# A softmax-attention block in eight wide steps in place of sixteen, and an output stage in another buffer

## The reference

```python
# recurrence
xp = silu(LN(x) @ W_in.T)
alpha, beta = sigmoid(xp @ W_alpha.T + b), sigmoid(xp @ W_beta.T + b)
h_t = alpha_t * h_(t-1) + (beta * tanh(xp @ W_v.T + b_v))_t
x = x + (h * silu(h)) @ W_out
# heads within a position: H = 16, HD = 64
y = LN(x); h = rmsnorm(y)
q = h @ Wq + bq; kv = (h @ Wdown + bdown) @ Wup + bup
att = softmax(q_h . k_g / 8 over the 16 heads g)     # per position
u = y + (att @ v) @ Wo + bo
# experts: E = 8
h2 = rmsnorm(u); gate = softmax(h2 @ Wg + bg)
x = x + u + sum_e gate_e * (h2 @ We_e)
```

## Time and profile before

| | us |
|---|---|
| median of 3 runs | 3924.3 (3923.45 to 3926.99) |
| the profiled execution's own time | 3921.82 |
| its span on the slowest core | 3919.9 |
| spans of the 8 cores | 3892.3 to 3919.9 |
| PE busy | 2538.4 (65%) |
| DVE busy | 1510.3 (39%) |
| ACT busy | 875.7 (22%) |
| mean granted TensorE clock of the slowest core | 0.762 of full |

### The profile page before, as it was taken

The page is one execution under the profiler, slowest core; times in us unless marked ns, Lnnn a source line. Parts: engine busy times, 40 slices in busy tenths (PEclk is TensorE's granted clock), DMA queues, the critical chain, the costliest instruction groups (busy, mean ns, idle before and its releaser), DMA issues.

```text
span 3919.9 us, 36774 instructions; the slowest of 8 cores (3892.3 to 3919.9 us)
## 1 busy us (share of the span) xinstructions
PE 2538.4 (65%) x12352; PEld 1190.4 (30%) x12352; DVE 1510.3 (39%) x2201; ACT 875.7 (22%) x1642; POOL 79.9 (2%) x143
## 2 busy tenths in 40 slices
PE   3555766557774487645975459664696647965478
PEld 1222332223332233222432224332243223432234
DVE  1353323443334433344324533146332363234532
ACT  2232003321123201332023320242203411023210
POOL 0000000000000000000000000000000000000000
PEclk8756888657886688966888669785698757987579
DMA  8631681201321022300223003220042201412012
GB/s 169 143 83 43 129 193 65 86 5 75 135 108 43 22 86 108 129 22 22 108 108 108 22 22 129 108 86 22 22 150 86 108 1 40 154 65 86 1 65 108
DMA packets 44465, 319.80 MB, mean 82 GB/s; under 512 B 5048, under 2 KB 5304, under 8 KB 28928
## 3 DMA queue, kind: packets, MB, share of 16 engines
q0 software_dynamic: 35040, 283.53, 23.1%
q1 hardware_dynamic: 9248, 33.91, 2.2%
HBM read 301.07 MB, written 48.23 MB: 89 GB/s over the span
## 4 chain that ended last, share of the span: by engine, by line
PE 52%; DVE 19%; DMA 10%; issue 7%; ACT 7%; DVEq 4%; ACTq 1%; POOL 0%; POOLq 0%; SPq 0%
PE bank L1420 21%; PE bank L614 3%; PE bank L836 3%; PE bank L1137 3%; DMA w<-wscr 3%; DMA w<-we 3%; PE bank L1363 3%; PE bank L443 3%; PE bank L489 2%; DVE vpu L927 2%; DVE kpot L927 2%; DVE xph L1036 2%; DVE sstat L1026 2%; PE bank L965 2%; DVEq L1030 2%
## 5 line engine op out<-in xcount | busy, mean ns | idle before, releaser
L1420 PE MATMUL bank<-qpg,w 128*128 128x512 bf16 x4096 | 915.6, 388 | 77.0 <-DVE qpg L1393 42.2
L1420 PEld LDWEIGHTS bank<-qpg,w 128*128 128x128 bf16 x4096 | 406.8, 100 | 594.5 <-issue 131.6
L1393 DVE TENSOR_TENSOR qpg<-xph,ybuf 128x4096 bf16<-128x4096 bf16 x64 | 282.4, 4423 | 502.2 <-PE bank L1420 502.2
L1012 ACT ACTIVATE hfm<-bank,sstat 128x128 bf16<-128x128 f32 x512 | 146.0, 368 | 652.7 <-DVE sstat L987 641.6
L1437 ACT ACTIVATE acomb<-bank 128x512 f32<-128x512 f32 x64 | 38.2, 597 | 1133.3 <-PE bank L1420 1129.4
L1059 PE MATMUL bank<-cpb_s,xph 128*128 128x128 bf16 x512 | 74.9, 300 | 332.1 <-DVE xph L1036 308.9
L525 PE MATMUL bank<-xph,w 128*128 128x512 bf16 x512 | 133.1, 407 | 125.5 <-DMA w<-wscr 64.9
L614 PE MATMUL bank<-ln1g,w 128*128 128x512 bf16 x512 | 128.5, 418 | 97.2 <-DMA w<-wscr 74.6
L987 DVE TENSOR_REDUCE sstat<-bank 128x4 f32<-128x512 f32 x128 | 88.5, 692 | 235.9 <-PE bank L965 235.9
L912 PE MATMUL bank<-zb,wupb 64*128 64x512 bf16 x128 | 73.2, 584 | 156.0 <-DVE vpu L927 112.0
L927 DVE TENSOR_SCALAR kpot<-bank,cph_s 64x512 bf16<-64x512 f32 x128 | 95.1, 743 | 196.5 <-PE bank L912 192.6
(11 more groups left out here) (139 smaller groups left out, 3025.4 us busy)
## 6 DMA issues: line engine op xcount, KB each, us to landing
w<-wscr POOLq DMA_DIRECT2D x105, 2048.0 KB, 8.1
wscr<-w POOLq DMA_DIRECT2D x15, 2048.0 KB, 9.3
w<-we POOLq DMA_DIRECT2D x8, 2048.0 KB, 20.2
out<-tmstage SPq DMA_DIRECT2D x16, 1024.0 KB, 4.0
slotA<-x SPq DMA_DIRECT2D x4, 2048.0 KB
slotB<-x SPq DMA_DIRECT2D x4, 2048.0 KB, 12.7
w<-w_inT POOLq DMA_DIRECT2D x1, 2048.0 KB, 29.3
w<-w_aT POOLq DMA_DIRECT2D x1, 2048.0 KB, 23.0
```

Source lines behind the costliest of these rows:

```text
L1012: last_s = s.activation(out=p1_[bb % 4][:, g4 * 128:(g4 + 1) * 128], in_=bkS[:, g4 * 128:(g4 + 1) * 128], func=AF.Exp, bias=sstat[:, SG_[b ...
L1393: r = v.tensor_tensor(qpg[:, (e % 2) * 4096:(e % 2) * 4096 + 4096] .rearrange("p (c q) -> p c q", q=512), h2v[:, :, :], ybuf[:, e * 512:(e ...
L1420: last_pe = pe.matmul(bk[:, :], wslice(wbuf, kc, mc), qpg[:, (e % 2) * 4096 + kc * 512: (e % 2) * 4096 + (kc + 1) * 512], start=(e == 0 an ...
```

## The change

A step of the attention block takes 8 groups in place of 4, so there are 8 blocks `mm` (`NMAC = 8`) and 12 steps. The scores of a block fill two banks: 0 and 1, or 2 and 3. P transposes take banks 4 and 5, V transposes bank 6 alone, O bank 7 over its whole width. Maxima stay two instructions, one to a bank; exponentials stay one to a group. V copy, sums, reciprocals, multiply, P copy and O copy become one instruction for 8 groups. Scores wait for the exponentials two blocks back (three before) and for V copy of the block before (two blocks back before). `p1_` has three slots of 1024, `p1n_` and `p1t_` two, and `vlay_` moves to the second half of `ln1g`. `stage2` becomes the first half of `ybuf`; the waits for the output transfer of the tile before go from the two writers of `tmstage` (L390, L785) to the three writers of `ybuf`.

```diff
-    p1_ = [hfm[:, i * 512:(i + 1) * 512] for i in range(4)]
-    p1n_ = [xph2[:, i * 512:(i + 1) * 512] for i in range(4)]
-    p1t_ = [xph2[:, 2048 + i * 512: 2048 + (i + 1) * 512] for i in range(2)]
-    vlay_ = [xph2[:, 3072 + i * 256: 3072 + (i + 1) * 256] for i in range(4)]
+    p1_ = [hfm[:, i * 1024:(i + 1) * 1024] for i in range(3)]
+    p1n_ = [xph2[:, i * 1024:(i + 1) * 1024] for i in range(2)]
+    p1t_ = [xph2[:, 2048 + i * 1024: 2048 + (i + 1) * 1024] for i in range(2)]
+    vlay_ = [ln1g[:, 2048 + i * 512: 2048 + (i + 1) * 512] for i in range(4)]
...
-    stage2 = tmstage[:, :].bitcast(F32)
+    stage2 = ybuf[:, 0:2048]
...
                 s.wait_ge(s_ve.h, tok[("ln1nmr", t)])
                 if t > 0:
-                    osem, oval = tok[("out", t - 1, 1)]
-                    s.wait_ge(osem.h, oval)
+                    s.wait_ge(s_pe.h, tok[("h2T", t - 1, NCH - 1)])
...
                     s.wait_ge(s_pe.h, tok[("wbv", t, mc)])
+                    if mc == 0 and t > 0:
+                        osem, oval = tok[("out", t - 1, 1)]
+                        s.wait_ge(osem.h, oval)
...
-                if t > 0:
-                    osem, oval = tok[("out", t - 1, 1)]
-                    s.wait_ge(osem.h, oval)
                 for b in range(NBLK):
                     last_s = s.activation(out=tmstage[:, b * 1024:(b + 1) * 1024],
...
                 s.wait_ge(s_ve.h, tok[("bv", t, NCH - 1)])
+                if t > 0:
+                    osem, oval = tok[("out", t - 1, 1)]
+                    s.wait_ge(osem.h, oval)
                 for b in range(NBLK):
                     last_s = s.activation(out=ybuf[:, b * 1024:(b + 1) * 1024],
...
+            def emit_F1(mm):
+                bkS = [banks[2 * (mm % 2)], banks[2 * (mm % 2) + 1]]
+                bkV = banks[6]
...
+                    if mm < 2:
                         pe.wait_ge(s_se.h, tok[("qe", t, NCH - 1)])
                         pe.wait_ge(s_ve.h, tok[("kve", t, 15)])
...
                     else:
+                        pe.wait_ge(s_se.h, tok[("p1e", t, mm - 2)])
+                    if mm >= 1:
+                        pe.wait_ge(s_ve.h, tok[("vle", t, mm - 1)])
+                    for half in range(2):
+                        bk = bkS[half]
+                        pe.matmul(bk[:, :], QM, KM, start=True, stop=False)
+                        for g4 in range(4):
...
+                    for g8 in range(8):
+                        grp = mm * 8 + g8
+                        last_pe = pe.transpose(bkVb[:, g8 * 64:(g8 + 1) * 64],
...
+                    for half in range(2):
+                        r = v.tensor_reduce(
+                            sstat[:, SG_[mm % 2] + 4 * half:SG_[mm % 2] + 4 * half + 4],
+                            bkS[half][:, :].rearrange("p (g n) -> p g n", n=128),
+                            axis=AX, op=OP.max, negate=True)
...
+                    r = v.tensor_copy(vlay_[mm % 4][:, :],
+                                      bkV[:, :].bitcast(BF16)[:, 0:512])
...
+                    if mm >= 3:
+                        s.wait_ge(s_ve.h, tok[("ssum", t, mm - 3)])
+                    for g8 in range(8):
+                        half, g4 = g8 // 4, g8 % 4
                         last_s = s.activation(
+                            out=p1_[mm % 3][:, g8 * 128:(g8 + 1) * 128],
+                            in_=bkS[half][:, g4 * 128:(g4 + 1) * 128],
...
+                        p1_[mm % 3][:, :].rearrange("p (g n) -> p g n", n=128),
                         axis=AX, op=OP.add)
...
+                    r = v.tensor_copy(p1t_[mm % 2][:, :],
+                                      bkP[:, :].bitcast(BF16)[:, 0:1024])
...
+                        if g8 == 3:
+                            s_pe.inc(last_pe)
+                            tok[("avh", t, mm)] = s_pe.n
...
+                        bkO[:, 0:512].rearrange("p (g u i) -> p g u i", u=8, i=8))
...
+            NMAC = 8
+            for step in range(NMAC + 4):
...
                         if e == 0:
                             dwait(v, "d_y")
                             v.wait_ge(s_ve.h, tok[("ud", t)])
+                            if t > 0:
+                                osem, oval = tok[("out", t - 1, 1)]
+                                v.wait_ge(osem.h, oval)
```

More of the change, by code:

```diff
@@ L136, in build_program @@
     S_GMAX, S_SSUM, S_RSUM = 44, 48, 52
-    SG_ = [64 + 4 * i for i in range(4)]
-    SS_ = [80 + 4 * i for i in range(4)]
-    SR_ = [96 + 4 * i for i in range(4)]
+    SG_ = [64, 72]
+    SS_ = [80, 88]
+    SR_ = [96, 104]
     banks = [ctx.enter_context(nc.psum_tensor(f"bank{i}", [128, 512], F32))
@@ L960, in f_s1 @@
                     else:
[L961 to L968, removed]
+                        pe.wait_ge(s_se.h, tok[("p1e", t, mm - 2)])
[5 more added lines that the diff above has]
+                        for g4 in range(4):
+                            grp = mm * 8 + half * 4 + g4
+                            last_pe = pe.matmul(bk[:, g4 * 128:(g4 + 1) * 128],
+                                      q64[:, grp * 128:(grp + 1) * 128],
+                                      k64[:, grp * 128:(grp + 1) * 128],
+                                      start=False, stop=(g4 == 3))
                     s_pe.inc(last_pe)
-                    tok[("s1", t, bb)] = s_pe.n
+                    tok[("s1", t, mm)] = s_pe.n
                     bkVb = bkV[:, :].bitcast(BF16)
-                    for g4 in range(4):
-                        grp = bb * 4 + g4
-                        last_pe = pe.transpose(bkVb[:, g4 * 64:(g4 + 1) * 64],
+                    for g8 in range(8):
+                        grp = mm * 8 + g8
+                        last_pe = pe.transpose(bkVb[:, g8 * 64:(g8 + 1) * 64],
                                      v64[:, grp * 128:(grp + 1) * 128],
@@ L1008, in f_exp @@
                         dwait(s, "d_hfm")
-                    if bb >= 4:
-                        s.wait_ge(s_ve.h, tok[("ssum", t, bb - 4)])
-                    for g4 in range(4):
+                    if mm >= 3:
+                        s.wait_ge(s_ve.h, tok[("ssum", t, mm - 3)])
+                    for g8 in range(8):
+                        half, g4 = g8 // 4, g8 % 4
                         last_s = s.activation(
-                            out=p1_[bb % 4][:, g4 * 128:(g4 + 1) * 128],
-                            in_=bkS[:, g4 * 128:(g4 + 1) * 128],
+                            out=p1_[mm % 3][:, g8 * 128:(g8 + 1) * 128],
+                            in_=bkS[half][:, g4 * 128:(g4 + 1) * 128],
@@ L1055, in f_p1tT @@
                     else:
-                        pe.wait_ge(s_ve.h, tok[("p1te", t, bb - 2)])
+                        pe.wait_ge(s_ve.h, tok[("p1te", t, mm - 2)])
                     bkPb = bkP[:, :].bitcast(BF16)
-                    for g4 in range(4):
-                        last_pe = pe.transpose(bkPb[:, g4 * 128:(g4 + 1) * 128],
-                                     p1n_[bb % 4][:, g4 * 128:(g4 + 1) * 128], idb)
+                    for g8 in range(8):
+                        last_pe = pe.transpose(bkPb[:, g8 * 128:(g8 + 1) * 128],
+                                     p1n_[mm % 2][:, g8 * 128:(g8 + 1) * 128], idb)
@@ L1084, in f_av @@
                     elif t > 0:
                         pe.wait_ge(s_ve.h, tok[("G", t - 1, 7)])
-                    for g4 in range(4):
+                    for g8 in range(8):
                         for hl in range(2):
                             last_pe = pe.matmul(
-                                bkO[64 * hl:64 * hl + 64, g4 * 64:(g4 + 1) * 64],
-                                vlay_[bb % 4][:, g4 * 64:(g4 + 1) * 64],
-                                p1t_[bb % 2][:, g4 * 128 + hl * 64:
-                                             g4 * 128 + (hl + 1) * 64],
+                                bkO[64 * hl:64 * hl + 64,
+                                    (g8 % 8) * 64:(g8 % 8) * 64 + 64],
+                                vlay_[mm % 4][:, g8 * 64:(g8 + 1) * 64],
+                                p1t_[mm % 2][:, g8 * 128 + hl * 64:
+                                             g8 * 128 + (hl + 1) * 64],
@@ L1110, in f_ote @@
                     s_ve.inc(r)
-                    tok[("ote", t, bb)] = s_ve.n
+                    tok[("ote", t, mm)] = s_ve.n
                 block.vector(f_ote)
-            for step in range(16 + 4):
-                if step < 16:
+            NMAC = 8
+            for step in range(NMAC + 4):
+                if step < NMAC:
                     emit_F1(step)
                     emit_F2(step)
-                if step >= 2 and step - 2 < 16:
+                if step >= 2 and step - 2 < NMAC:
@@ L1119, in build_program @@
                     emit_B1(step - 2)
-                if step >= 4 and step - 4 < 16:
+                if step >= 4 and step - 4 < NMAC:
                     emit_B3(step - 4)
-                if step >= 3 and step - 3 < 16:
```

(3 more changed lines are left out.)

157 lines of the change are left out of this document (68 added, 89 removed).

## The result

The changed kernel takes 3841.58 us (median of nine runs), the kernel before 3922.37 us (ten runs): a ratio of 0.9793, 95% interval 0.9777 to 0.981. The prediction was 3841, range 3805 to 3868. The profiled execution took 3847.39 us; its cores' spans run from 3809.3 to 3845.4 us.

A forecast was written before the change was run, and what follows sets the result against it. The attention block was taken as a loop passing between VectorE and TensorE, neither engine the bound; 10.45 us less a tile, 83.6 in eight, took 3921.8 to 3838.2, plus 2.5 for the median: 3841, range 3805 to 3868.

The forecast's parts named there:

- VectorE's half: Attention block, steady step: VectorE's work from the maxima on takes 5.58 us, for 6.48 in two old steps.
- TensorE's half: Attention block, steady step: from the P copy's end to the next maxima 3.32 us, for 4.04 in two old steps.
- Head and tail: Attention block's start and end: maxima 7 at 54.18 us, then 18.20 to the output projection, 72.38 in all for 82.83.
- The added wait of scores 1 for V copy 0: Attention block's head: with one bank for V transposes, scores 1 wait for V copy 0 and start at 4.19 us.
- ScalarE: Attention block: eight exponentials take 2.3 us, covered, no scores delayed; otherwise each 1 us late costs 1 us a step.
- The output stage's move: Layer norm of the next tile: it loses its wait for the output DMA, gain nothing, covered by the sum over x.
- The total: Whole kernel: 83.6 us off the profiled 3921.8 gives 3838.2; the median stands 2.5 higher, so 3841; chance 0.80.
- a stage outside the block that changes length: Outside the attention block: any stage changing length was named as showing the prediction wrong; no size given.
- (a): Attention block: wider bursts release TensorE's clock, scores and PV get cheaper, 9 us a tile, so 3769; chance 0.10.
- (b): Attention block: everything doubles with the width, 1.6 us less a tile, 3911; 3896 if only VectorE doubles; chance 0.05.
- (c): Weight loads in each tile: a shorter block makes them meet and take twice as long, so 3979; chance 0.03.
- (d): Behind the attention block: another wait takes the gain and the time stays at 3924; chance 0.02.

The follow-up runs named there:

- the reordered wide kernel: The changed kernel with TensorE's scores and V transposes of step k+1 issued ahead of P transposes k-2 and PV k-3; ratio 0.942 to the kernel before.
- the last version: The reordered wide kernel with V copy and O copy moved from VectorE to ScalarE; ratio 0.9309 to the kernel before.
- the narrow kernel in the new order: The kernel before, sixteen narrow steps, with TensorE's scores and V transposes of block k+1 issued ahead of P transposes and PV; ratio 0.9556.

## Why the prediction was right, step by step

**VectorE's half.** Predicted 5.58 us, measured 5.59. The widened instructions came out as the two-size estimate had them. Groups of the changed kernel (line, operation, count, total busy and mean ns), which answer to the earlier trace rows:

```profile
L1040 DVE TENSOR_TENSOR xph<-hfm,sstat 128x1024 bf16<-128x1024 bf16 x64 | 78.4, 1225 | 8.4 <-issue 0.4
...
L1030 DVE TENSOR_REDUCE sstat<-hfm 128x8 f32<-128x1024 bf16 x64 | 77.4, 1210 | 0.0
...
L1115 DVE CAST tmstage<-bank 128x512 bf16<-128x512 f32 x64 | 43.9, 686 | 17.7 <-PE bank L1092 17.7
L1077 DVE COPY xph<-bank 128x1024 bf16<-128x1024 bf16 x64 | 43.6, 682 | 0.0
```

Multiply 1.225 us (estimated 1.22), sums 1.21 (1.21), O copy 0.686 and P copy 0.682 (0.69 each). That the fixed part is what was saved here is shown by the kernel with narrow VectorE instructions: 0.71 us a step for six instructions more. The Trainium skill (VectorE: DVE Perf Modes, the section on the TRN2 errata) says that VectorE operations reading SBUF pay a fixed extra latency in each instruction, and so many small ones pay it many times. The trace agrees that there is a fixed part, but not that it comes with reading SBUF: two narrow multiplies, which read SBUF, last 0.15 us longer than the wide one (2 x 0.69 and 1.23), two narrow P copies, which read PSUM, 0.16 longer (2 x 0.42 and 0.68), and by starts they cost 0.08 and 0.06 more.

**TensorE's half.** Predicted 3.32, measured 3.32, but that is luck: two terms were off by as much in opposite directions. PV to the next scores was twice the old 0.35, 0.71, and measured 0.57 (1287.05 to 1287.62): two PV bursts back to back cost less than two apart. Scores to the maxima was 2.25 (2.08 and the hand-over of 0.17), and measured 2.39 (1287.62 to 1290.01). The first half's four score matmuls are followed by the next mask matmul after 0.53 us; I had priced them at 0.40, the time until a V transpose follows.

**Head and tail.** From the first score matmul (1244.86), predicted then measured: maxima 0 at 2.25, 2.30; maxima 2 at 10.63, 10.50; maxima 4 at 27.48, 27.33; maxima 7 at 54.18, 54.05; tail 18.20, 17.98. The added wait of scores 1 for V copy 0 is there, and it is as long as worked out. Timeline of the changed kernel: start of the block, scores 1, the last maxima and the output projection, answering to the earlier trace rows:

```profile
1244.86 0.58 PE L964 MATMUL bank<-cpb_s 8*128 8x512 bf16 x1 [2.61 <-DVE vpu L929]
...
1248.93 0.58 PE L964 MATMUL bank<-cpb_s 8*128 8x512 bf16 x1 [1.45 <-DVE ln1g L999]
...
1298.91 0.69 DVE L990 TENSOR_REDUCE sstat<-bank 128x4 f32<-128x512 f32 x1 [3.31 <-PE bank L967]
...
1316.89 1.44 PE L1146 MATMUL bank<-tmstage,w 128*128 128x512 bf16 x3 [1.05 <-DVE tmstage L1115]
```

The block is 72.03 us, predicted 72.38. Scores 1 start 4.07 after the first, predicted 4.19, by a hand-over of 0.15 from the V copy's end (1248.78) where I took 0.30.

**ScalarE.** The exponentials took 2.18 us and stopped no scores: the bracket in front of the scores of a steady step is empty. Predicted at nothing, and nothing it was.

**The output stage's move.** Predicted at nothing, covered by the sum over x. In the changed kernel the application comes 7.36 us after the sum's start, as before, and alone the move gives a ratio of 1.0.

**The total.** The forecast was 83.6 us off the profiled time, 3838.2, and with the median's 2.5 on top 3841. The blocks gave 87.6, 4.0 more: 0.28 a tile because the new block is shorter than the sum, 0.22 because the mean old block, 83.05, is longer than tile 2's 82.83. The span of the slowest core fell by only 74.5. The difference lies outside the blocks. On that core the stretch from the end of tile 0's block to the start of tile 1's took 454.76 us, and 443.37 on the slowest core of the kernel before, 11.4 more. Most of this is in expert weight loads, which the chains show one behind the other. First the changed kernel's, then those of the kernel before:

```profile
411.47 16.99 DMA w<-we
429.70 22.52 DMA w<-we
```

```profile
421.25 17.10 DMA w<-we
439.59 20.68 DMA w<-we
```

With the third to the sixth, left out above (23.55, 22.50, 23.22 and 23.18 us, against 20.43, 20.06, 21.01 and 21.86), the six sum to 131.96 and 121.14 us, 10.8 more. Only tile 0 has such loads: it takes the weights from the given arrays (`w<-we`, median 22.5 us a load), the later tiles from a copy that the kernel has made (`w<-wscr`, 8.1). It is largely a matter of which core one looks at: the same stretch runs from 426.3 to 454.8 us over the cores of the changed kernel and from 427.1 to 443.4 in the kernel before. The means over all eight cores are 438.2 and 434.4; the repeated change gives 438.2, the output stage alone 436.2, and the other kernels 434.8 to 443.3.

In later tiles the stretch is 392.57 us where it was 391.94, 0.63 more in each of six (means over the cores). Of this 0.57 has come about by the time the experts' matmuls start, 67.85 us behind the block's end in place of 67.28. The larger part is the output projection right behind the block. TensorE starts it at a granted clock of 0.50, and the clock goes to 1.00 later in it than before: 4.2 us after its start in the mean over cores and tiles, 3.4 in the kernel before. In tile 2 the window that begins 2.1 us after its start was granted 0.84 before and 0.72 in the change (below). The projection takes 15.92 us in place of 15.53 (means over the cores and tiles 1 to 7); the 0.39 more are about half of the 0.8 by which the clock comes later. The other kernels go the same way: 3.5 us and 15.58 with the output stage alone, 4.6 and 16.18 in the reordered wide kernel, 5.2 and 16.54 with narrow VectorE instructions.

Means over the cores account for the spans. The blocks gave 87.3. The stretch after tile 0's block took 3.8 back, the six later ones 3.8, what lies ahead of the first block and behind the last 1.2 together. That leaves 78.5, and the mean span fell by 78.5 (3905.1 to 3826.6). So the forecast's sum had two terms mis-sized: 4 us of gain too little in the blocks, and 9 us of cost outside them that it put at nothing. They offset in part, and the 5 us that are left are within what single executions of the change scatter (3833.03 to 3849.51 us); that the median comes within 1 us of 3841 is luck. The prediction also named a stage outside the block that changes length as a sign of being wrong. That sign came true, for the output projection, and is worth 3 us of 87.

**The rivals.** (a) *Clock released*: refuted. The clock was 0.50 in the block, with TensorE busy for 3.21 of 3.40 us, and it stayed there in the reordered kernel, where TensorE is busy 62% of the block. No block of any core in the ten traces was granted more. It rises only behind the block, in gapless work of the output projection, here in tile 2. Windows of the changed kernel, which answer to the earlier trace rows:

```profile
1316.90:1320.30 3.40, 3.40 (x9) 1.17 (x10) 0.00 (x0) 0.00 (x0) 0.00 (x0) 0.50 0.00 0
1319.00:1322.40 3.40, 3.40 (x13) 1.38 (x12) 0.00 (x0) 0.69 (x1) 0.00 (x0) 0.72 0.00 0
1322.40:1325.80 3.40, 3.40 (x18) 1.50 (x17) 0.00 (x0) 1.38 (x2) 0.00 (x0) 1.00 0.00 0
```

The Trainium skill (TensorE: Matmul & The Clock Gate, the section on the HAM clock gate) has activity release the clock; the trace agrees in the projection, and in the block it did not happen in any kernel of this study. (b) *No fixed costs saved*: refuted for the change, and its milder end, where only hand-overs are saved, was built: 78.0 us a block. The prediction's 3896 was for this case, and a ratio of 0.9935 to its 3924 is 3899. (c) *Weight loads collide*: not seen in steady tiles. Chain of the changed kernel, tile 2, which answers to the earlier trace rows:

```profile
1144.06 9.68 DMA w<-wscr
```

The longer one, shown, took 9.93 before; the other takes 8.15. Even in the last version, with blocks of 47.6 us, they take 8.3 and 10.3 us. Only in tile 0, where six loads are on the path one behind the other, is there a difference of that kind. (d) *Swallowed*: refuted, the gain of the blocks reaches the end.

**What stays open.** Whether the 3.8 us more after tile 0's block is the change's or scatter between executions. The repeated change (438.2) speaks for the first, and the reordered wide kernel (434.8), with a still shorter block, against it; so does the narrow kernel in the new order, which has none of the change in it and 439.2. Why the clock rises later behind the wide block was not tried apart. It isn't the width alone: in the narrow kernel with the new order it rises after 4.0 us, and the later stretches are 392.7. They differ among wide kernels, too: 392.5 to 393.6, and 393.4 in the wide steps with the old output stage, against 391.9 in both kernels with the old attention block.

## What to carry to other kernels

In a loop that passes between two in-order engines, write down one period as a sum of work on either side and two hand-overs; a wider step divides the hand-overs and the fixed part of every instruction, most of it at instructions that the program drains before it reads their result (0.22 us each here, 0.06 to 0.08 at the others), and leaves the rest. Then ask whether the serial half has to be there at all: here widening alone gave 2.1%, moving one engine's independent matmuls ahead of its dependent ones alone 4.4%, for a few lines of code, and both together 5.8%. The new order makes new waits, so look which single buffer is now written beside its last reader. When a term of such a sum is a burst repeated twice, take its follower from a row with the same follower: the price of four score matmuls here changed from 0.40 to 0.53 us with what came next.

## What was not expected of the hardware

- A stretch with TensorE busy for 3.21 of 3.40 us, and whole blocks of 54.8 us with 34.05 busy, kept a granted clock of 0.50. The projection directly behind, gapless, was at 0.50 for its first 3.4 us and at 1.00 from 1322.4 on.
- Sixteen PV matmuls in one burst took 0.57 us until the next instruction's start, where eight took 0.35; and score matmuls of 4 x 128 columns took 0.53 us ahead of a mask matmul of 512 columns, 0.40 ahead of a V transpose.
- The second to the sixth expert weight load, all of one size and one behind the other on the path, took from 20.1 to 23.6 us each in tile 0 of two executions, and the stretch that holds these loads differed by 28 us between cores of one execution.
